# A graph network kernel: score factors stored once and doubled by the loads, and the projection stage in another order

## The chip, the cores and the metric

The kernel runs on one core of a Trainium2 chip. The metric is the device time of one execution in microseconds (us); before the change the median of three runs is 1293.65 us (1293.31 to 1293.77).

## The reference, cut to what matters

3125 nodes with 96 channels pass through four blocks, each added to its input. The change touches the first block, attention along the edges, and what feeds it. All four blocks start with the same layer norm and a ReLU:

```python
h = jnp.maximum(_layernorm(x, axis=-1), 0.0)
x = x + _L0_gnn_ref(h, qW, kW, vW, src, dst)
# _L0_gnn_ref: 4 heads of 24 channels, one row per edge
q = (embeds[rows] @ qW).reshape(e, HEADS, dh)
k = (embeds[cols] @ kW).reshape(e, HEADS, dh)
v = (embeds[cols] @ vW).reshape(e, HEADS, dh)
scores = jnp.clip(jnp.einsum('ehd,ehd->eh', q, k), -10.0, 10.0)
exp_s = jnp.exp(scores)
norms = jax.ops.segment_sum(exp_s, rows, num_segments=nvar)[rows]
w = exp_s / (norms + 1e-08)
res = jax.ops.segment_sum(w[:, :, None] * v, rows, num_segments=nvar).reshape(nvar, d)
return embeds + res
```

The kernel doesn't gather edges here. It has a matrix CT that counts the edges between each pair of nodes, forms the scores of all pairs, and weighs the exponentials with the counts. The column sums of CT (the degrees) are needed by later blocks and by the edge softmax.

## The kernel before, in words

Five engines run their own instruction streams, written out by hand; between stages all five meet (`meet`), so a stage ends for everybody when its last engine, or the last transfer that SyncE waits for, is done. The stages are: build (CT is made), projection, attention, propagation, last. Nothing in the streams is reordered by a planner: within an engine the order is that of the calls in `proj_tensor`, `proj_scalar`, `proj_vector` and `proj_sync`, and semaphores tie the engines together.

Projection works on 7 blocks of 512 nodes (the last has 64), of 4 tiles of 128 nodes each. Its pieces, with their lines in the kernel before:

- `dst_rows(b)` (L872): 25 matmuls sum CT's columns of block b into a PSUM bank; `rows(b)` on ScalarE (L811) copies it out; `dst_sums(b)` (L880) turns it to one column a tile in bank 6. After the seventh, `keep_degrees` (VectorE) copies the degrees, two matmuls (L916, L917) make running sums, and `last_edges` (L758 to L771, VectorE) makes an index of them.
- the layer norm on VectorE: `stats` (L704), `variances` (L709, L711) for all 25 tiles at once, the square root on ScalarE (L837, which needs a table load), the reciprocal (L788), and `norm(b)` (L717 and L720), which makes hb and adds ReLU(h) to X.
- `turn(b)` (L862) transposes hb to channels by nodes; `h_copy(b)` (L817, ScalarE) keeps it with the ReLU.
- `scales` (VectorE, L726 to L746) finds a power of two for the weights from `w_norm` (L903) and writes wqk.
- `products(b)`: Q and K of block b (L890), the values (L896).
- each Q or K block is split in a high fp16 part (`highs`, ScalarE, L825) and a low one, the rest (`low`, VectorE, L777). The score matmul contracts over 96 rows: 4 groups of 24, whose products are high·high, high·low, low·high and low·low. So DRAM holds four parts of each block, and `store` (L669, SyncE) writes each part twice: 4 transfers a block of 192 KB, Q ordered high, high, low, low, K ordered high, low, high, low. QH has two buffers: `highs(b)` waits until the stores of block b-2 have landed.
- X with ReLU(h) goes to DRAM (x1_d) in two stores (L682), after block 0 and after block 4.

Attention has 7 destination blocks by 25 source tiles, 175 steps. SyncE loads Q of a block (`q_load`, L1004) and K of each step (`k_load`, L1011) into a ring of three. One step is four score matmuls (L1064), ScalarE's exponentials (L1115 to L1119), floor and cap on GpSimd and VectorE (L982, L1144, L1150), and four value matmuls (L1074).

Of the kernel before, what the change touches and what calls it, by code (L numbers as in the profile page):

```python
# [4 lines left out]
F32 = mybir.dt.float32  # L5
# [645 lines left out]
def proj_sync(q, K):  # L651
# [13 lines left out]
    q.dma_start(K.wv4[:, :], K.vW).then_inc(S("wv4_in"), 16)  # L665
    def store(to, b, n, i):

        wb = width(b)
        q.dma_start(to.rearrange("r c h w -> (c h) r w")[:, :, 0:wb], bcast_out(K.QH[:, b % 2, n, i, 0:wb], 2, wb)  # L669
                    ).then_inc(S("q_out%d" % (b % 2)), 16)  # L670

    for b in range(7):
        q.wait_ge(S("q_low"), 2 * b + 1)
        for i in range(2):
            store(K.qd[b, 2 * i:2 * i + 2], b, 0, i)
        q.wait_ge(S("q_low"), 2 * b + 2)
        for i in range(2):
            store(K.kd[b, i:4:2], b, 1, i)
# [5 lines left out]
    q.wait_ge(S("q_out0"), 64 * 4)  # L684
    q.wait_ge(S("q_out1"), 64 * 3)


def proj_vector(v, K):
# [16 lines left out]

    def variances():
        v.wait_ge(step, own.n)
        for t in range(NT):
            v.bn_aggr(K.mv[:, t, :], K.bns[:, t, :]).then_inc(step, own.up())  # L709
        v.wait_ge(step, own.n)  # L710
        v.tensor_scalar(K.rs[:, 0, :], K.mv[:, :, 1], 1e-5, None, ALU.add).then_inc(S("ln0_var"), 1)  # L711

    def norm(b):

        sl = slice(4 * b, 4 * b + tiles(b))
        for t in range(4 * b, 4 * b + tiles(b)):
            c = v.tensor_scalar(K.hb[:, t, :], K.X[:, t, :], K.mv[:, t, 0:1], K.rs[:, 2, t:t + 1], ALU.subtract, ALU.mult)  # L717
        c.then_inc(S("h0"), 1)
        v.wait_ge(S("h0"), b + 1)
        v.scalar_tensor_tensor(out=K.X[:, sl, :], in0=K.hb[:, sl, :], scalar=0.0, in1=K.X[:, sl, :], op0=ALU.max, op1=ALU.add  # L720
                               ).then_inc(S("x1"), 1)

    def scales():

        v.wait_ge(S("w_norm"), 1)
        v.tensor_reduce(sc[:, 0, :], K.bank(3)[:, 0:192].rearrange("p (n c) -> p n c", n=2), AX.X, ALU.max  # L726
                        ).then_inc(step, own.up())
# [57 lines left out]
    variances()  # L785
    scales()
    v.wait_ge(S("ln0_std"), 1)
    v.reciprocal(K.rs[:, 2, :], K.rs[:, 1, :]).then_inc(step, own.up())  # L788
    v.wait_ge(step, own.n)
    norm(0)  # L790
    norm(1)
    norm(2)
# [11 lines left out]
def proj_scalar(a, K):  # L804
    S = K.S

    def rows(b):
        a.wait_ge(S("dst_rows"), b + 1)
        if b >= 2:
            a.wait_ge(S("dst_deg"), b - 1)  # L810
        a.activation(K.RD[:, b % 2, 0:width(b)], K.bank((7, 4)[b % 2])[:, 0:width(b)], ACT.Copy).then_inc(S("rows_kept"), 1)  # L811

    def h_copy(b):
        a.wait_ge(S("h_turned"), b + 1)
        if b >= 2:
# [20 lines left out]
    a.wait_ge(S("ln0_var"), 1)
    a.activation(K.rs[:, 1, :], K.rs[:, 0, :], ACT.Sqrt).then_inc(S("ln0_std"), 1)  # L837
    rows(3)
    rows(4)
    rows(5)  # L840
    h_copy(0)
    rows(6)
    h_copy(1)
    for b in range(7):
        highs(b)
        values(b)
        if b + 2 < 7:
            h_copy(b + 2)
    a.wait_ge(S("v_kept"), 7)


def proj_tensor(t, K):
    S, bank = K.S, K.bank

    def turn(b):
        t.wait_ge(S("h0"), b + 1)
        if b == 1:
            t.wait_ge(S("w_set"), 2)
        if b >= 2:
            t.wait_ge(S("hT"), b - 1)  # L860
        for i in range(tiles(b)):
            m = t.transpose(bank((0, 3)[b % 2])[0:96, 128 * i:128 * i + 128], K.hb[:, 4 * b + i, :], K.identf[:, :])  # L862
        m.then_inc(S("h_turned"), 1)

    def dst_rows(b):

        wb = width(b)
        if b >= 2:
            t.wait_ge(S("rows_kept"), b - 1)
        for a in range(NT):  # L870
            j = a % 4
            m = t.matmul(bank((7, 4)[b % 2])[32 * j:32 * j + 32, 0:wb], K.ones32[:, :], K.CT[:, a, 512 * b:512 * b + wb],  # L872
                         start=(a < 4), stop=(a >= NT - 4), tile_position=(0, 32 * j))
        m.then_inc(S("dst_rows"), 1)
# [9 lines left out]
    def products(b):  # L884
# [9 lines left out]
        for i in range(tiles(b)):  # L894
# [24 lines left out]
    turn(2)  # L919
    for b in range(1, 7):  # L920
        products(b)
        if b + 2 < 7:
            turn(b + 2)
    t.wait_ge(S("v_made"), 7)
# [118 lines left out]
def attn_tensor(p, K):  # L1043
# [966 lines left out]
```

## Time and profile before

| | us |
|---|---|
| median of the three runs | 1293.65 |
| profiled execution, device time | 1290.73 |
| span of its trace | 1288.6 |
| PE, DVE, ACT, POOL busy | 1040.7, 967.3, 692.3, 598.5 |
| projection stage | from 358.3 to 406.9 |
| attention stage | from 406.9 to 874.3 |

PE is the matmul engine (TensorE), PEld its weight loads, DVE VectorE, ACT ScalarE, POOL GpSimd, SP SyncE, which only issues transfers here. The profiled execution is 2.9 us shorter than the median of the runs. The projection is 3.8% of the span, so the shares of the page say little on it: it has to be read from windows of its own.

### The profile page before, as it was taken

How to read it: one execution, taken by the hardware profiler on the slowest of the kernel's cores; microseconds unless marked ns; L12 is line 12 of the kernel's file. 1: busy time of each engine (PE TensorE's matmuls, PEld its weight loads, DVE VectorE, ACT ScalarE, POOL GpSimd, SP SyncE). 2: the span in 40 equal slices, each digit the busy share in tenths (PEclk: the TensorE clock that was granted, in tenths of full speed). 3: DMA queues.
4: the chain of work that ended last, by engine and by line, in shares of the span. 5: the costliest groups of instructions: out<-in, count | busy, mean ns of one | idle time of the engine just before them, and what ended most of it. 6: DMA issues, size and time to landing. Idle time of an engine off the chain costs nothing.

```text
span 1288.6 us, 23338 instructions
## 1 busy us (share of the span) xinstructions
PE 1040.7 (81%) x8352; PEld 615.1 (48%) x8352; DVE 967.3 (75%) x1603; ACT 692.3 (54%) x903; POOL 598.5 (46%) x343
## 2 busy tenths in 40 slices
PE   3877777777795888888888888882799699999893
PEld 2545545544452222222222222221469699999783
DVE  8668888897764999999999999981865654542566
ACT  7555566556534997999989999980000000001221
POOL 8542453232001998999999899996000000000000
PEclk9988888999987998999999999996799899999996
DMA  0010000000027111121111222211000100010201
GB/s 10 28 39 5 5 9 5 6 7 16 1 63 213 35 36 46 44 54 41 42 47 45 51 54 50 53 41 46 1 1 32 37 29 21 2 33 8 71 25 38
DMA packets 98907, 44.80 MB, mean 35 GB/s; under 512 B 85196, under 2 KB 96716, under 8 KB 98672
## 3 DMA queue, kind: packets, MB, share of 16 engines
q1 hardware_dynamic: 97104, 41.58, 12.2%
q0 software_dynamic: 1696, 1.74, 0.5%
q8 instruction: 74, 1.21, 0.4%
q14 instruction: 33, 0.27, 0.1%
HBM read 30.73 MB, written 12.56 MB: 34 GB/s over the span
## 4 chain that ended last, share of the span: by engine, by line
PE 51%; DVE 25%; issue 11%; ACT 5%; POOL 5%; another core or an unknown queue 2%; DMA 2%; SPq 1%; DVEq 0%; ACTq 0%; POOLq 0%
PE PS L1325 16%; DVE Eb L1150 16%; PE PS L553 10%; PE PS L557 8%; POOL Eb L982 3%; PE PS L1765 3%; DVE Eb L1144 3%; PE PS L1333 2%; PE PS L1074 2%; ACT Eb L1115 2%; PE PS L1064 2%; PE PS L1316 1%; ACT Eb L1117 1%; PE PS L1772 1%
## 5 line engine op out<-in xcount | busy, mean ns | idle before, releaser
L982 POOL TENSOR_SCALAR Eb<-Eb 128x1024 f32<-128x1024 f32 (+4 forms) x175 | 431.2, 2486 | 77.1 <-ACT Eb L1119 75.8
L1150 DVE SCALAR_TENSOR_TENSOR Eb<-Eb,PS 128x1024 f32<-128x1024 f32 (+4 forms) x350 | 366.6, 1084 | 18.0 <-ACT Eb L1117 11.7
L1119 ACT ACTIVATE Eb<-PS,small 128x1024 f32<-128x1024 f32 (+2 forms) x263 | 251.7, 998 | 28.9 <-PE PS L1064 25.2
L593 ACT ACTIVATE CT<-PS 128x500 f32 x313 | 183.6, 587 | 141.2 <-PE PS L557 132.6
L553 PE MATMUL PS<-mov,oneS 128*128 128x100 f16 x1565 | 182.2, 226 | 79.6 <-issue 74.0
L553 PEld LDWEIGHTS PS<-mov,oneS 128*128 128x128 f16 x1565 | 144.7, 104 | 157.9 <-issue 111.5
L1325 PE MATMUL PS<-hs,CT 128*128 128x192 f16 (+1 forms) x2500 | 213.9, 247 | 3.5 <-DVE SG L1566 1.6
L1325 PEld LDWEIGHTS PS<-hs,CT 128*128 128x128 f16 (+1 forms) x2500 | 208.4, 99 | 7.4 <-DVE SG L1566 2.3
L1064 PE MATMUL PS<-Qb,Kb 96*128 96x512 f16 (+3 forms) x700 | 184.5, 367 | 10.4 <-ACT Eb L1119 6.7
L1074 PE MATMUL PS<-Eb,V 128*25 128x512 f32 (+3 forms) x1400 | 172.6, 566 | 3.4 <-DVE Eb L1150 1.8
L435 DVE TENSOR_TENSOR oneS<-iotaX,KL 128x2560 f16<-128x2560 int16 x80 | 120.8, 1510 | 68.7 <-PE PS L557 67.0
L1064 PEld LDWEIGHTS PS<-Qb,Kb 96*128 96x128 f16 (+1 forms) x700 | 45.3, 99 | 200.1 <-ACT Eb L1119 148.9
L557 PE MATMUL PS<-CT,identb 128*128 x313 | 137.7, 440 | 1.3 <-ACT CT L593 0.9
L1053 PE MATMUL PS<-identb,CT 128*128 128x128 f16 (+1 forms) x625 | 68.9, 225 | 59.7 <-DVE Eb L1150 51.4
L1053 PEld LDWEIGHTS PS<-identb,CT 128*128 128x128 f16 (+1 forms) x625 | 39.1, 100 | 129.1 <-DVE Eb L1150 114.3
L435 DVE TENSOR_TENSOR mov<-iotaM,KL 128x2000 f16<-128x2000 int16 x80 | 98.2, 1228 | 0.0
L1115 ACT ACTIVATE Eb<-PS,small 128x1024 f32<-128x1024 f32 (+4 forms) x87 | 95.1, 1093 | 0.0
L1117 ACT ACTIVATE Eb<-Eb,small 128x1024 f32<-128x1024 f32 (+4 forms) x87 | 90.7, 1043 | 2.8
L217 POOL TENSOR_SCALAR key<-hi 120x128 f32<-120x128 int32 x14 | 8.8, 630 | 173.8 <-DVE hi L444 173.7
L1446 ACT ACTIVATE hs<-PS 96x96 f32<-96x96 f32 x9 | 2.2, 248 | 138.8 <-PE PS L1357 138.8
L1566 DVE TENSOR_REDUCE SG<-PS 128x96 f32<-128x192 f32 (+1 forms) x75 | 24.8, 352 | 60.7 <-PE PS L1325 60.4
L1144 DVE TENSOR_SCALAR Eb<-Eb 128x1024 f32<-128x1024 f32 (+4 forms) x88 | 63.2, 718 | 7.4 <-ACT Eb L1119 7.4
(278 smaller groups left out, 1007.2 us busy)
## 6 DMA issues: line engine op xcount, KB each, us to landing
Kb<-kd SPq DMA_DIRECT2D x168, 96.0 KB, 2.3
qd<-QH SPq DMA_DIRECT2D x12, 192.0 KB, 2.9
kd<-QH SPq DMA_DIRECT2D x12, 192.0 KB, 3.2
hs<-t_d SPq DMA_DIRECT2D x12, 192.0 KB, 2.5
Qb<-qd SPq DMA_DIRECT2D x4, 384.0 KB, 3.9
CT<-x_d SPq DMA_DIRECT2D x1, 1200.0 KB, 9.1
x_d<-B SPq DMA_DIRECT2D x6, 192.0 KB, 1.9
t_d<-A SPq DMA_DIRECT2D x6, 192.0 KB, 1.9
```

Source lines behind the costliest of these rows:

```text
L435: return v.tensor_tensor(out.rearrange("p e (c two) -> p e c two", two=2), v_in, k_in, ALU.is_equal)
L553: t.matmul(to, K.oneS[:, s % DEEP, o + k, :], K.mov[:, s % DEEP, o + k, :].rearrange("p (a w) -> p a w", a=25), start=(k == 0), stop=False ...
L557: t.matmul(ps, K.identb[:, :], K.CT[:, :, bass.ds(vals[0], GI * W)], start=False, stop=True, skip_group_check=True).then_inc(S("counted"), 1)
L593: a.activation(K.CT[:, :, bass.ds(words[g % 4][0], GI * W)], K.bank(g % 4)[:, 0:25 * GI * W].rearrange("p (a c) -> p a c", a=25), ACT.Copy ...
L982: g.tensor_scalar(e, e, ELO, None, ALU.max).then_inc(S("floored"), 1)
L1053: m = p.transpose(K.cntv[it % 2][0:r, 128 * i:128 * i + w], K.CT[0:w, B0[b] + i, 128 * t:128 * t + r], K.identb[0:w, 0:w])
L1064: m = p.matmul(bank(h)[0:r, 0:wb], K.Kb[:, it % NK, h, 0:r], K.Qb[:, b % 2, h, 0:wb], start=True, stop=True)
L1074: m = p.matmul(bank(4)[32 * h:32 * h + 25, 0:wb], K.V[0:r, t, h, :], K.Eb[0:r, (2 * it + h // 2) % NE_, h % 2, 0:wb], start=(t == 0), stop ...
L1115: a.activation(e, ps, ACT.Relu, bias=K.ten[0:r, 0:1], scale=K.unsc[0:r, :]).then_inc(S("score_read"), 1)
L1119: a.activation(e, ps, ACT.Exp, scale=K.unsc[0:r, :]).then_inc(S("score_read"), 1)
L1150: v.scalar_tensor_tensor(out=e, in0=e, scalar=EHI, in1=cn, op0=ALU.min, op1=ALU.mult).then_inc(S("weighed"), 1)
L1325: m = p.matmul(bank(t % FIRST)[0:r, 0:w], K.CT[:, a, 128 * t:128 * t + r], hs[:, a, :, :].rearrange("p k d -> p (k d)"), start=(a == 0), s ...
```

## The change

1. DRAM holds two parts of each Q or K block instead of four: the high once and the low once (`qd`, `kd` of 7 x 2 x 24 x 4 x 512). A block is stored in 2 transfers of 192 KB, not 4.
2. The loads make the doubling: Q in four transfers of 24 partitions a piece, not one of 96, K in two of 48 partitions a step, not one of 96. A wait for K is for 32 and not 16.
3. QH has three buffers.
4. The layer norm goes in three portions (tiles 0 to 3, 4 to 11, 12 to 24), each with its own variances, square root and reciprocal. hb is a ring of 16 tiles.
5. The column sums are placed between the blocks' products on TensorE, with one PSUM bank (3), not two; the transposes have bank 0 alone.
6. `scales` comes after `norm(0)`; `keep_degrees` and `last_edges` come behind `low(4)`; the two x1 stores come after blocks 3 and 6.

The core of the diff:

```diff
-    K.hb = sb(st, "hb", [128, NT, D], F32)
+    K.hb = sb(st, "hb", [128, 16, D], F32)
-    K.QH = sb(st, "QH", [96, 2, 2, 2, 512], F16)
+    K.QH = sb(st, "QH", [96, QH_DEEP, 2, 2, 512], F16)
...
+QH_DEEP = 3
-    def store(to, b, n, i):
+    def store(to, b, n):
-        q.dma_start(to.rearrange("r c h w -> (c h) r w")[:, :, 0:wb], bcast_out(K.QH[:, b % 2, n, i, 0:wb], 2, wb)
-                    ).then_inc(S("q_out%d" % (b % 2)), 16)
+        q.dma_start(to.rearrange("i c h w -> (c h) i w")[:, :, 0:wb], K.QH[:, b % QH_DEEP, n, :, 0:wb]
+                    ).then_inc(S("q_out%d" % (b % QH_DEEP)), 16)
-        if b in (0, 4):
-            lo, hi = (0, 12) if b == 0 else (12, NT)
-            q.wait_ge(S("x1"), 3 if b == 0 else 7)
+        if b in (3, 6):
+            lo, hi = (0, 12) if b == 3 else (12, NT)
+            q.wait_ge(S("x1"), 3 if b == 3 else 7)
...
     stats(0)
+    variances(0)
     v.wait_ge(S("w_in"), 32)
     v.tensor_tensor(K.wsq[:, :, :], wr, wr, ALU.mult).then_inc(S("w_sq"), 1)
+    deviations(0)
+    norm(0)
+    scales()
     stats(1)
+    variances(1)
+    deviations(1)
+    norm(1)
+    low(0)
+    norm(2)
     stats(2)
...
+    low(4)
     keep_degrees()
+    norm(6)
     last_edges()
-    for b in range(7):
-        low(b)
-        if b + 3 < 7:
-            norm(b + 3)
+    low(5)
+    low(6)
...
+    deviation(0)
     rows(0)
+    h_copy(0)
+    deviation(1)
+    highs(0)
     rows(1)
+    values(0)
+    h_copy(1)
+    deviation(2)
+    highs(1)
...
+    for b in (1, 2):
+        dst_rows(b)
+        turn(b)
+        dst_sums(b)
+        products(b)
+    for b in (3, 4):
+        dst_rows(2 * b - 3)
+        turn(b)
+        dst_sums(2 * b - 3)
+        dst_rows(2 * b - 2)
+        products(b)
+        dst_sums(2 * b - 2)
...
-            q.dma_start(K.Qb[:, b % 2, :, o:o + w], K.qd[c // 512].rearrange("r c h w -> (r c) h w")[:, :, c % 512:c % 512 + w]
-                        ).then_inc(S("q_in%d" % (b % 2)), 16)
+            for r in range(4):
+                q.dma_start(K.Qb[24 * r:24 * r + 24, b % 2, :, o:o + w], K.qd[c // 512, r // 2, :, :, c % 512:c % 512 + w]
+                            ).then_inc(S("q_in%d" % (b % 2)), 16)
...
-        q.dma_start(K.Kb[:, it % NK, :, 0:r], K.kd[t // 4].rearrange("r c h w -> (r c) h w")[:, :, 128 * (t % 4):128 * (t % 4) + r]
-                    ).then_inc(S("k_in%d" % (it % NK)), 16)
+        kt = K.kd[t // 4].rearrange("i c h w -> (i c) h w")[:, :, 128 * (t % 4):128 * (t % 4) + r]
+        for i in range(2):
+            q.dma_start(K.Kb[48 * i:48 * i + 48, it % NK, :, 0:r], kt).then_inc(S("k_in%d" % (it % NK)), 16)
```

ScalarE at the start of the projection, kernel before: RD is the copied column sums, rs the square root's tile, hTb the turned block, and the brackets name the semaphores waited for.

```order
L811 ACTIVATE RD<-PS 128x512 [waits placed,dst_rows,meet]
L811 ACTIVATE RD<-PS 128x512 [waits dst_rows]
L811 ACTIVATE RD<-PS 128x512 [waits dst_deg,dst_rows]
L837 ACT_TABLE_LOAD
L837 ACTIVATE rs<-rs 128x25 [waits ln0_var]
```

The same place now (L859 is the square root, L834 the copy of the sums, L840 `h_copy`, L848 `highs`):

```order
L859 ACT_TABLE_LOAD [waits placed,ln0_var]
L859 ACTIVATE rs<-rs 128x4 [waits meet]
L834 ACTIVATE RD<-PS 128x512 [waits dst_rows]
L840 ACTIVATE hTb<-PS 96x512 [waits h_turned]
L859 ACTIVATE rs<-rs 128x8 [waits ln0_var]
L848 ACTIVATE QH<-PS 96x512 [waits q_made] x2
```

The table load stood by itself and waited for nothing; now it is the first instruction of the stage and carries the wait for the first variances. Each later square root stands ahead of a `highs`.

VectorE at the stage's end, now (L764 and L766 are `keep_degrees`, L731 and L734 `norm(6)`, L772 to L785 `last_edges`, L791 `low`):

```order
L764 COPY small<-PS 128x24 [waits dst_deg]
L766 COPY small<-PS 64x1 [waits step_v]
L731 TENSOR_SCALAR hb<-X,mv,rs 128x96 [waits h_turned]
L734 SCALAR_TENSOR_TENSOR X<-hb,X 128x96 [waits h0]
L772 COPY bns<-PS 128x25 [waits deg_sum]
L773 COPY bns<-PS 128x25
L785 TENSOR_SCALAR msk<-small 128x25
L791 TENSOR_TENSOR QH<-PS,QH 96x512 [waits q_high] x2
L791 TENSOR_TENSOR QH<-PS,QH 96x64 [waits q_high] x2
```

Before, the degrees and the index were done ahead of the first `low`; now they stand ahead of the last two, behind a wait for TensorE.

SyncE around the meeting, now (L675 is `store`, L686 the x1 store, L1046 `q_load`, L1055 `k_load`):

```order
L675 DMA qd<-QH 96x2x64 [waits q_low]
L675 DMA kd<-QH 96x2x64 [waits q_low]
L686 DMA x_d<-X 128x1248 [waits x1]
L1046 DMA Qb<-qd 24x2048 [waits q_out2,q_out1,x1_out,q_out0,meet]
L1046 DMA Qb<-qd 24x2048 x3
L1055 DMA Kb<-kd 48x4x128 x6
```

The larger x1 store has become the stage's last transfer, and the first K load now has four Q issues ahead of it instead of one.

## Rows read from the trace of the kernel before

**Rows 1.** Windows of the projection: PE, PEld, DVE, ACT, POOL busy, clock, DMA, GB/s.

```profile
358.00:364.00 6.00, 5.21 (x51) 2.23 (x51) 2.43 (x18) 0.84 (x2) 0.50 (x2) 0.59 0.74 189
364.00:384.00 20.00, 20.00 (x217) 13.72 (x217) 14.37 (x84) 9.13 (x16) 0.00 (x0) 1.00 0.04 11
384.00:397.00 13.00, 11.58 (x57) 6.90 (x57) 9.98 (x25) 6.54 (x14) 0.00 (x0) 1.00 0.90 277
397.00:407.00 10.00, 1.75 (x14) 1.32 (x13) 1.71 (x7) 1.92 (x6) 0.00 (x0) 0.67 0.81 247
```

**Rows 2.** Waits in the projection: us in total, times, longest.

```profile
ACT QH L825 <- DMA kd<-QH: 6.0, 4, 2.5
```

**Rows 3.** Transfers issued in the projection: count, KB each, us to landing.

```profile
qd<-QH SPq DMA_DIRECT2D x12, 192.0 KB, 2.9
x_d<-X SPq DMA_DIRECT2D x1, 624.0 KB, 5.0
wv<-in_L_gnn_vW SPq DMA_DIRECT2D x1, 36.0 KB, 4.3
```

**Rows 4.** Timeline of TensorE in the projection: start, us, engine, line.

```profile
358.79 5.18 PE L872 MATMUL PS<-CT,ones 128*32 128x512 f16 x50 [1.25 <-DVE sel L695]
...
365.21 1.69 PE L872 MATMUL PS<-CT,ones 128*32 128x512 f16 x25
366.82 1.05 PE L880 MATMUL PS<-sel,RD 128*128 128x1 f32 x8
...
381.00 0.62 PE L862 MATMUL PS<-identf,hb 128*96 128x128 f32 x4
381.46 1.88 PE L890 MATMUL PS<-hTb,wqk 96*96 96x512 f32 x4
383.18 1.03 PE L896 MATMUL PS<-wv,hTb 96*128 96x96 f32 x8
```

**Rows 5.** Timeline of ScalarE: the table loads and what follows one.

```profile
367.55 1.28 ACT L837 ACT_TABLE_LOAD   x1
...
411.88 1.28 ACT L1119 ACT_TABLE_LOAD   x1 [9.60 <-PE PS L1064]
413.18 1.11 ACT L1119 ACTIVATE Eb<-PS,small 128x1024 f32<-128x1024 f32 x1
```

**Rows 6.** Timeline of VectorE in the projection.

```profile
360.74 0.74 DVE L704 BATCH_NORM_STATS2 bns<-X 128x6 f32<-128x96 f32 x4 [1.76 <-DMA X<-in_x]
...
370.47 0.35 DVE L726 TENSOR_REDUCE sc<-PS 128x2 f32<-128x192 f32 x1
...
372.07 0.51 DVE L742 TENSOR_SCALAR wqk<-wr,sc 96x96 f32<-96x96 f32 x2
...
373.09 1.05 DVE L717 TENSOR_SCALAR hb<-X,mv,rs 128x96 f32<-128x96 f32 x4
...
381.20 0.18 DVE L758 COPY bns<-PS 128x25 f32<-128x25 f32 x1 [2.90 <-PE PS L917]
...
382.61 1.28 DVE L777 TENSOR_TENSOR QH<-PS,QH 96x512 f16<-96x512 f32 x2
```

**Rows 7.** Timeline of SyncE after the meeting.

```profile
406.87 0.32 SPq L1004 DMA_DIRECT2D Qb<-qd  x1
407.23 1.97 SPq L1011 DMA_DIRECT2D Kb<-kd  x3
```

**Rows 8.** Timeline of TensorE: the first scores.

```profile
410.75 1.89 PE L1064 MATMUL PS<-Qb,Kb 96*128 96x512 f16 x4 [1.80 <-DMA Kb<-kd]
```

**Rows 9.** Transfers of the whole run: count, KB each, us to landing.

```profile
Kb<-kd SPq DMA_DIRECT2D x168, 96.0 KB, 2.3
x_d<-B SPq DMA_DIRECT2D x6, 192.0 KB, 1.9
```

**Rows 10.** Waits of SyncE in attention: us in total, times, longest.

```profile
SPq L1011 <- PE PS L1064: 323.9, 165, 6.6
```

**Rows 11.** Score matmuls: count, ns min/median/max, first and last start.

```profile
L1064 PE MATMUL PS<-Qb,Kb x700: 298/379/634, 410.8 to 864.0; 96*128 96x512 f16 x96, 96*128 96x384 f16 x48, 96*128 96x320 f16 x24, 96*64 96x512 f16 x4
```

More of the change, by code:

```diff
@@ L704, in stats, with variances, deviations @@
             v.bn_stats(K.bns[:, t, :], K.X[:, t, :]).then_inc(step, own.up())
-    def variances():
+    def variances(i):
+        lo, hi = X_IN[i]
         v.wait_ge(step, own.n)
-        for t in range(NT):
+        for t in range(lo, hi):
             v.bn_aggr(K.mv[:, t, :], K.bns[:, t, :]).then_inc(step, own.up())
         v.wait_ge(step, own.n)
-        v.tensor_scalar(K.rs[:, 0, :], K.mv[:, :, 1], 1e-5, None, ALU.add).then_inc(S("ln0_var"), 1)
+        v.tensor_scalar(K.rs[:, 0, lo:hi], K.mv[:, lo:hi, 1], 1e-5, None, ALU.add).then_inc(S("ln0_var"), 1)
+    def deviations(i):
+        lo, hi = X_IN[i]
+        v.wait_ge(S("ln0_std"), i + 1)
+        v.reciprocal(K.rs[:, 2, lo:hi], K.rs[:, 1, lo:hi]).then_inc(step, own.up())
+        v.wait_ge(step, own.n)
     def norm(b):
         sl = slice(4 * b, 4 * b + tiles(b))
+        ring = slice(4 * (b % 4), 4 * (b % 4) + tiles(b))
+        if b >= 4:
+            v.wait_ge(S("h_turned"), b - 3)
         for t in range(4 * b, 4 * b + tiles(b)):
-            c = v.tensor_scalar(K.hb[:, t, :], K.X[:, t, :], K.mv[:, t, 0:1], K.rs[:, 2, t:t + 1], ALU.subtract, ALU.mult)
+            c = v.tensor_scalar(K.hb[:, t % 16, :], K.X[:, t, :], K.mv[:, t, 0:1], K.rs[:, 2, t:t + 1], ALU.subtract, ALU.mult)
         c.then_inc(S("h0"), 1)
         v.wait_ge(S("h0"), b + 1)
-        v.scalar_tensor_tensor(out=K.X[:, sl, :], in0=K.hb[:, sl, :], scalar=0.0, in1=K.X[:, sl, :], op0=ALU.max, op1=ALU.add
+        v.scalar_tensor_tensor(out=K.X[:, sl, :], in0=K.hb[:, ring, :], scalar=0.0, in1=K.X[:, sl, :], op0=ALU.max, op1=ALU.add
                                ).then_inc(S("x1"), 1)
@@ L776, in low @@
             v.wait_ge(S("q_high"), 2 * b + n + 1)
-            v.tensor_tensor(K.QH[:, b % 2, n, 1, 0:wb], K.bank(qk_bank(b, n))[0:96, 0:wb], K.QH[:, b % 2, n, 0, 0:wb],
+            v.tensor_tensor(K.QH[:, b % QH_DEEP, n, 1, 0:wb], K.bank(qk_bank(b, n))[0:96, 0:wb], K.QH[:, b % QH_DEEP, n, 0, 0:wb],
                             ALU.subtract).then_inc(S("q_low"), 1)
     stats(0)
+    variances(0)
     v.wait_ge(S("w_in"), 32)
     v.tensor_tensor(K.wsq[:, :, :], wr, wr, ALU.mult).then_inc(S("w_sq"), 1)
+    deviations(0)
+    norm(0)
+    scales()
     stats(1)
-    stats(2)
[L785 to L792, printed above, removed]
+    variances(1)
[3 more added lines that the diff above has]
+    norm(2)
+    stats(2)
+    variances(2)
+    low(1)
+    deviations(2)
+    norm(3)
+    low(2)
+    norm(4)
+    low(3)
+    norm(5)
+    low(4)
     keep_degrees()
+    norm(6)
     last_edges()
-    for b in range(7):
-        low(b)
-        if b + 3 < 7:
-            norm(b + 3)
+    low(5)
+    low(6)
     v.wait_ge(S("q_low"), 14)
@@ L816, in h_copy @@
             a.wait_ge(S("v_made"), b - 1)
-        a.activation(K.hTb[:, b % 2, 0:width(b)], K.bank((0, 3)[b % 2])[0:96, 0:width(b)], ACT.Relu).then_inc(S("hT"), 1)
+        a.activation(K.hTb[:, b % 2, 0:width(b)], K.bank(0)[0:96, 0:width(b)], ACT.Relu).then_inc(S("hT"), 1)
     def highs(b):
@@ L831, in values, with deviation @@
                      K.bank(5)[0:r, 0:96 * n].rearrange("p (k c) -> p k c", c=24), ACT.Copy).then_inc(S("v_kept"), 1)
+    def deviation(i):
+        lo, hi = X_IN[i]
+        a.wait_ge(S("ln0_var"), i + 1)
+        a.activation(K.rs[:, 1, lo:hi], K.rs[:, 0, lo:hi], ACT.Sqrt).then_inc(S("ln0_std"), 1)
+    deviation(0)
     rows(0)
+    h_copy(0)
+    deviation(1)
+    highs(0)
     rows(1)
+    values(0)
+    h_copy(1)
+    deviation(2)
+    highs(1)
     rows(2)
[L836 to L844, printed above, removed]
-        highs(b)
-        values(b)
-        if b + 2 < 7:
-            h_copy(b + 2)
+    values(1)
+    h_copy(2)
+    highs(2)
+    for b in (3, 4):
+        rows(2 * b - 3)
+        values(b - 1)
+        h_copy(b)
+        rows(2 * b - 2)
+        highs(b)
+    for b in (5, 6):
+        values(b - 1)
+        h_copy(b)
+        highs(b)
+    values(6)
     a.wait_ge(S("v_kept"), 7)
@@ L856, in turn @@
         t.wait_ge(S("h0"), b + 1)
[L857 to L860, printed above, removed]
+        if b:
+            t.wait_ge(S("hT"), b)
         for i in range(tiles(b)):
-            m = t.transpose(bank((0, 3)[b % 2])[0:96, 128 * i:128 * i + 128], K.hb[:, 4 * b + i, :], K.identf[:, :])
+            m = t.transpose(bank(0)[0:96, 128 * i:128 * i + 128], K.hb[:, 4 * (b % 4) + i, :], K.identf[:, :])
         m.then_inc(S("h_turned"), 1)
@@ L900, in proj_tensor @@
     dst_rows(0)
-    dst_rows(1)
     t.wait_ge(S("w_sq"), 1)
-    t.matmul(bank(3)[:, 0:192], K.ones96[:, :], K.wsq[:, :, :].rearrange("p n c -> p (n c)"), start=True, stop=True
+    t.matmul(bank(7)[:, 0:192], K.ones96[:, :], K.wsq[:, :, :].rearrange("p n c -> p (n c)"), start=True, stop=True
              ).then_inc(S("w_norm"), 1)
-    for b in range(2, 7):
-        dst_sums(b - 2)
-        dst_rows(b)
     turn(0)
-    dst_sums(5)
-    turn(1)
-    dst_sums(6)
+    dst_sums(0)
+    t.wait_ge(S("w_set"), 2)
     t.wait_ge(S("wv4_in"), 16)
     products(0)
+    for b in (1, 2):
[3 more added lines that the diff above has]
+        products(b)
+    for b in (3, 4):
+        dst_rows(2 * b - 3)
[4 more added lines that the diff above has]
+        dst_sums(2 * b - 2)
+    turn(5)
+    products(5)
+    turn(6)
     t.wait_ge(S("tri"), 1)
@@ L918, in proj_tensor @@
              ).then_inc(S("deg_sum"), 1)
[L919 to L923, printed above, removed]
+    products(6)
     t.wait_ge(S("v_made"), 7)
@@ L970, in q_loaded @@
 def q_loaded(b):
-    return 16 * sum(len(list(q_pieces(i))) for i in range(b % 2, b + 1, 2))
+    return 64 * sum(len(list(q_pieces(i))) for i in range(b % 2, b + 1, 2))
 def attn_gpsimd(g, K):
```

30 lines of the change are left out of this document (14 added, 16 removed).

## The prediction

> **What bounds the kernel now.** The change lies in one stage and its seam to the next, so I read windows first. From 364 to 384 TensorE is busy 20.00 of 20 us while DMA moves 11 GB/s; from 384 on DMA is busy 90% at 277 GB/s, and in the last ten microseconds TensorE works 1.75 [rows 1]. The projection thus has two halves with different limits: first TensorE (column sums), then the stores of the score factors. The waits name the second: ScalarE's `highs` stand 6.0 us, in four waits, for stores of two blocks earlier to land [rows 2]. Six full blocks bring 24 stores of 192 KB, of which the Q half is one row [rows 3]. The stage ends at 406.87, when SyncE issues the first load [rows 7], and the first score starts at 410.75, having waited for K [rows 8].
>
> **The stores: what they can give.** Half of them go: 12 of 192 KB for the six full blocks, 2.3 MB, 8.3 us at 277 GB/s [rows 1]. But the gain ends where another engine ends. TensorE's work in the stage is 5.21 + 20.00 + 11.58 + 1.75 = 38.5 us [rows 1], from 358.8 on [rows 4], so 397.3 without a gap. So a gain of some 5 us after a tail of 4 us is what a dense TensorE would allow, and the question is whether the new order keeps it dense. It doesn't at its start, as the following shows.
>
> **The start.** Before, `products(0)` stood behind all column sums, so VectorE's norm and weight scaling had 19 us. Now they stand before it. The first statistics end at 361.48 [rows 6]; four aggregations and the addition of the 1e-5 take about 0.5, so 362.0. There ScalarE's table load begins, because it now carries the wait for the variances; it takes 1.28 and was hidden before [rows 5]. Square root about 0.2, reciprocal 0.2: `norm(0)` starts at 363.8. It takes 1.05 for the tiles and 0.56 for X. Then `scales`: from its first reduction at 370.47 to the start of wqk at 372.07 are 1.6, and two scalings 0.4 [rows 6]. The weights are set at 367.4. Vw is not later: issued near 362.3, it takes 4.3 [rows 3]. TensorE meanwhile has the first sums of columns (until 361.4: 25 of the 50 matmuls that take 5.18), the weight norm, one transposition and one `dst_sums`, at the low clock some 2.8 us of the 6.0 between 361.4 and 367.4. It idles over 3 us, where it idled nowhere before.
>
> **The rest of TensorE's chain.** Durations by start to start, at the high clock: `dst_rows` 1.61, `dst_sums` 0.98 (its row shows 1.05 with the end overlapped), a turn 0.46, Q and K 1.72 [rows 4]; values 0.87 (the row's 1.03 less the 0.16 by which the 1.88 of Q and K runs over too). Left after 367.4: six full products 15.5 and the small one 0.6; five and a bit `dst_rows` 8.4; sums 5.2; turns 2.5; the degree products 0.4 (half a `dst_sums`). Sum 32.6. To that come waits for ScalarE: with one bank for the turn and one for the sums, `dst_sums` follows its rows' copy (0.6) with only a turn to cover it, 0.3 in each of four blocks, and `products(5)` waits 0.8 for its own `h_copy`, the last 0.2. Sum 2.1. The clock: in the window 358 to 364 it is 0.59 (mostly 1.2 GHz), and 1.00 (2.4 GHz) after it; 50 matmuls at the low level took 5.18 where 25 at the high took 1.61 [rows 1, 4]. It was low while those first 50 ran, 358.8 to 364.0. I take a low stretch as long again once work is dense, 367.4 to near 372: half of it, 2.3, is lost. TensorE ends at 367.4 + 32.6 + 2.1 + 2.3 = 404.4. The blocks' stores are far from that: two of 192 KB in 6 to 8 us.
>
> **The tail.** `last_edges` waits for the degree products, which stand just before the last products, so they end at 403.6. It takes 1.41 (381.20 to 382.61), and behind it on VectorE wait `low(5)` and `low(6)`, 1.28 and 0.3 [rows 6]: 406.6. Behind these on SyncE are the last three stores, each about 0.45 to issue, and then the x1 store of 624 KB, issued at 407.7. It took 5.0 to land before, in a full queue [rows 3]; 192 KB in an empty one takes 1.9 [rows 9], and 432 KB more at 277 GB/s 1.6: 3.5, between 3.0 and 5.0. The stage would end at 411.2. The same layout by hand for the old order puts `products(0)` 0.4 later than the trace has it; I take that off: 410.8, against 406.87: **+3.9** (+1 to +8).
>
> **The start of attention.** Before, the Q load (0.32) and K loads of 0.66 each preceded a first score 3.88 after the first issue [rows 7, 8]. Now K's two halves stand behind four Q issues: 0.32 and three of 0.43 to 0.6, then 0.6 twice. The last one needed is issued 1.3 to 2.2 later than before; four transfers also deliver sooner in part. I take **+1.5** (+0.7 to +2.5), near the low end, since empty queues show 0.32.
> The Trainium skill, "DMA: Bandwidth & Descriptors", section "Why a DMA increments its semaphore by 16 and not by 1", says that a transfer uses the largest number of engines up to 16 that divides its slowest dimension: 12 for 24 partitions, where 96 had 16. No row here shows one of 24; by it the Q loads would last a third longer, at most 0.5 more, inside the range given.
>
> **Attention itself.** A step lasts (864.0 - 410.8) / 174 = 2.60 us [rows 11]. SyncE waits 323.9 us in 165 of its K issues, 1.96 each [rows 10]. The second K issue (0.6) fits. A load goes out three steps before its use, 7.8, and needs 1.2 to issue and 2.3 to land [rows 9], so 3 us are to spare even when a Q load of four or eight issues (2 to 4 us) comes between; with eight, in the narrow blocks, about one may show. I take 0, up to +3.
>
> **Other edits at nothing.** Three QH buffers: the two-block distance is now over 12 us against a landing of 3, the third buffer is never needed. The smaller hb ring waits for turns four blocks old. The first x1 store lies beside products.
>
> **A rule that speaks against this working.** A table load in the trace takes 1.28 and the exponential starts 0.02 after its end [rows 5]. The Trainium skill, "ScalarE: Activation LUTs", section "What ACT_TABLE_LOAD costs", adds a drain of 1.38. By it `products(0)` and the sum would move by another 1.4; the trace doesn't show a drain here, so I leave it out.
>
> **Sum.** 3.9 + 1.5 = 5.4. On the profiled execution, 1290.73, that is 1296.1; the runs' median is 2.9 above it, and 1293.65 + 5.4 = **1299.1**.
>
> **Rivals.**
> *A, faster: TensorE stays dense.* If norm, weights and copies came as TensorE needed them, it would end at 397.3, the tail (two stores, x1) at 401.7, and with +1.5 at the seam the kernel would gain 3.7: 1290.0. For it: the halved stores free 8 us that the waits prove. Against: the weights at 367.4 rest on five rows. It decides when idle at the start falls below about 1 us and `last_edges` ends before `highs(5)`. 0.07.
> *B, no change that can be measured.* The order costs as laid out, but clock and tail each come out at their kind ends (no cold products 2.3, the x1 store in 3.0, seam 0.7): 5.4 - 2.3 - 0.5 - 0.8 = 1.8, 1295.5. 0.14.
> *C, slower by more: the low clock holds.* The stage's new order leaves short pauses in each block. If the clock rises only near 380, another 4 us: 1303. For it: the low clock at this same place before, and 0.67 where work is thin [rows 1]. Against: after 367.4 hardly a pause is over 0.3. 0.11.
> *D, K loads late in attention.* If the doubled issues and the Q bursts use up the 3 us, each of six block changes shows 0.5 to 1: 1303 too. Against: the 1.96 of slack in each step. 0.06.
> *Forecast* 0.62, own range 1297 to 1301.5.
>
> The measurement of this kernel can tell about 0.2%, 2.6 us, from no change. Faster is A: 0.07; the same is B: 0.14; slower is the forecast with C and D: 0.79. The range for 8 in 10 reaches from 1295 (into B) to 1303.5.
>
> **What would show it.** In the new trace: the table load starting near 362 behind the variances; `products(0)` starting near 367.4 with TensorE idle some 3 us before it; a clock below 1 until about 372; TensorE ending near 404, two `low` blocks behind `last_edges`, an x1 store as the last transfer; `highs` no longer waiting for any store; the first attention issue near 410.8 and the first score 5.4 after it. A first issue at or before 406.9 would refute the stage's part, a score less than 4 after the first issue the seam's.

## The result, and the profile after

The changed kernel takes 1298.82 us in the median of six runs, against 1293.48 for the kernel before on the same chip: a ratio of 1.0049 (95% interval 1.0036 to 1.0061), 5.3 us slower. The prediction was 1299.1. All ratios here are of fast runs; this leaves out one run of the experiment "changed, filled", which took 4942 us.

The profiled execution took 1297.89 (span 1296.0). One cut of the trace into stages runs through all that follows: the projection from its first load of X to the first load of Q, the seam from there to the first score, attention from there to the next stage's first load.

| us | before | after | |
|---|---|---|---|
| build, up to the first load of X | 358.32 | 357.44 | -0.88 |
| projection | 48.55 | 55.31 | +6.76 |
| seam | 3.88 | 4.52 | +0.64 |
| attention | 463.59 | 464.42 | +0.83 |
| the rest | 414.26 | 414.31 | +0.05 |

The windows of the projection answer to [rows 1], with the same columns:

```profile
358.00:364.00 6.00, 4.06 (x27) 1.43 (x26) 2.64 (x16) 1.97 (x3) 0.04 (x1) 0.50 0.81 216
364.00:384.00 20.00, 19.58 (x113) 11.88 (x114) 15.77 (x78) 6.23 (x13) 0.00 (x0) 0.70 0.15 41
384.00:397.00 13.00, 12.77 (x126) 7.69 (x124) 5.78 (x14) 5.44 (x11) 0.00 (x0) 1.00 0.33 105
397.00:407.00 10.00, 8.68 (x73) 5.82 (x72) 3.31 (x16) 5.36 (x13) 0.00 (x0) 1.00 0.16 44
```

DMA, busy 90% from 384 to 397 before, is at 33%, and TensorE is at work to the end, where it had 1.75 of ten microseconds. TensorE's sum of busy time in these windows grew from 38.5 to 45.1 for the same work, mainly since it ran longer at the low clock. The timeline of TensorE shows where (to be read beside [rows 4]):

```profile
357.91 3.15 PE L907 MATMUL PS<-CT,ones 128*32 128x512 f16 x25 [1.25 <-DVE sel L699]
361.65 1.01 PE L937 MATMUL PS<-wsq,ones 96*128 96x192 f32 x2 [0.60 <-DVE wsq L797]
364.27 1.09 PE L897 MATMUL PS<-identf,hb 128*96 128x128 f32 x4 [1.61 <-DVE hb L731]
365.15 1.71 PE L915 MATMUL PS<-sel,RD 128*128 128x1 f32 x8
366.90 3.73 PE L925 MATMUL PS<-hTb,wqk 96*96 96x512 f32 x4
370.42 1.86 PE L931 MATMUL PS<-wv,hTb 96*128 96x96 f32 x8
372.21 3.17 PE L907 MATMUL PS<-CT,ones 128*32 128x512 f16 x25
375.31 0.97 PE L897 MATMUL PS<-identf,hb 128*96 128x128 f32 x4
376.11 1.00 PE L915 MATMUL PS<-sel,RD 128*128 128x1 f32 x8
376.98 1.94 PE L925 MATMUL PS<-hTb,wqk 96*96 96x512 f32 x4
...
402.21 1.96 PE L925 MATMUL PS<-hTb,wqk 96*96 96x512 f32 x4 [0.68 <-ACT hTb L840]
...
405.71 0.55 PE L925 MATMUL PS<-hTb,wqk 96*96 96x64 f32 x4 [0.22 <-ACT hTb L840]
```

The same Q and K products take 3.73 at 366.90 and 1.94 at 376.98; the column sums of block 1 (372.21) take 3.17, where 25 such matmuls took 1.69 at the high clock before. Windows date the rise of the clock (columns as above, the granted clock third from the end):

```profile
368.00:372.00 4.00, 4.00 (x12) 2.34 (x10) 3.58 (x20) 1.28 (x3) 0.00 (x0) 0.50 0.02 6
372.00:376.00 4.00, 4.00 (x31) 1.60 (x30) 3.97 (x19) 0.58 (x2) 0.00 (x0) 0.50 0.35 98
376.00:380.00 4.00, 4.00 (x30) 2.70 (x32) 2.51 (x18) 2.31 (x6) 0.00 (x0) 1.00 0.00 0
```

So TensorE stood at 1.2 GHz (0.50) up to 376, 18.6 us into the stage. Before, it left that level 4.5 us into it, near 362.9: the 0.59 of the window from 358 to 364 [rows 1] is 4.9 us at 0.50 and 1.1 at 1.00. ScalarE's start shows the table load behind the wait for the variances (compare [rows 5]):

```profile
361.42 1.28 ACT L859 ACT_TABLE_LOAD   x1 [4.06 <-DVE rs L716]
362.72 0.21 ACT L859 ACTIVATE rs<-rs 128x4 f32<-128x4 f32 x1
```

And the stage's end, VectorE and then SyncE (compare [rows 6, 7]):

```profile
405.54 0.18 DVE L772 COPY bns<-PS 128x25 f32<-128x25 f32 x1 [3.62 <-PE PS L962]
...
406.95 1.54 DVE L791 TENSOR_TENSOR QH<-PS,QH 96x512 f16<-96x512 f32 x4
```

```profile
407.65 0.30 SPq L675 DMA_DIRECT2D qd<-QH  x1
408.25 0.30 SPq L675 DMA_DIRECT2D kd<-QH  x1
408.60 0.48 SPq L675 DMA_DIRECT2D qd<-QH  x1
409.12 0.48 SPq L675 DMA_DIRECT2D kd<-QH  x1
409.65 0.45 SPq L686 DMA_DIRECT2D x_d<-X  x1
412.75 1.52 SPq L1046 DMA_DIRECT2D Qb<-qd  x4
414.31 3.88 SPq L1055 DMA_DIRECT2D Kb<-kd  x6
```

`last_edges` starts when the degree products are done (405.54), the last two blocks' `low` come behind it, and the x1 store closes the stage; all engines wait for it. Among the waits of the stage none is left of `highs` for a store. The largest of TensorE's waits are the ones in brackets above.

### The profile page after: what moved, and what is told of

Read it like the earlier page. It is cut to its first block, busy times and chain, and to the rows that moved or that the text cites. A ratio compares the mean times of both kernels' runs of the same rounds, so it can differ in the third digit from the quotient of the medians.

```text
span 1296.0 us, 23530 instructions
## 1 busy us (share of the span) xinstructions
PE 1047.7 (81%) x8352; PEld 617.8 (48%) x8352; DVE 967.1 (75%) x1607; ACT 693.3 (54%) x905; POOL 598.0 (46%) x343
## 4 chain that ended last, share of the span: by engine, by line
PE 50%; DVE 26%; issue 11%; ACT 5%; POOL 5%; another core or an unknown queue 2%; DMA 1%; SPq 0%; DVEq 0%; ACTq 0%; POOLq 0%
DVE Eb L1193 16%; PE PS L1368 16%; PE PS L553 10%; PE PS L557 7%; POOL Eb L1023 3%; DVE Eb L1187 3%; PE PS L1808 3%; PE PS L1376 2%; PE PS L1117 2%; ACT Eb L1158 2%; PE PS L1107 2%; PE PS L1359 1%; ACT Eb L1160 1%; PE PS L925 1%
```

## The experiments

Each kernel is compared with the kernel before on the same chip. The stage lengths come from one profile each. The build stage, the same in all of these, lasted from 357.4 to 362.9 in thirteen profiles, so whole times differ by microseconds that have nothing to do with the change; the projection of the changed kernel was 55.31 and 55.77 in two profiles. What varies in it is the moment at which the clock rises: 16.6 to 19.5 us into the stage in the five profiles that share the changed kernel's start. Half of that span, about 1.5 us, is an estimate of how far such a stage can move by itself.

| | ratio to before (95%) | projection | seam | attention |
|---|---|---|---|---|
| before | | 48.55 | 3.88 | 463.6 |
| changed | 1.0049 (1.0036 to 1.0061) | 55.31 | 4.52 | 464.4 |
| old order, parts once | 0.9978 (0.9962 to 0.9994) | 42.35 | 4.54 | 462.8 |
| changed, filled | 1.0056 (1.0034 to 1.0078) | 52.36 | 4.64 | 462.3 |
| changed, table first | 1.0051 (1.0034 to 1.0068) | 53.50 | 4.55 | 462.5 |
| changed, tail | 1.0034 (1.0013 to 1.0056) | 51.39 | 4.56 | 464.8 |
| changed, old storage | 1.0058 (1.0040 to 1.0077) | 57.30 | 3.91 | 460.7 |
| changed, two buffers | one run | 54.73 | 4.60 | 462.4 |
| changed, all three mended | 1.0021 (1.0003 to 1.0039) | 50.18 | 4.55 | 462.1 |
| the same, and unlocked | 0.9988 (0.9967 to 1.0010) | 45.83 | 4.46 | 462.6 |
| changed, again | one run | 55.77 | 4.49 | 464.2 |
| old order and three edits | 0.9970 (0.9953 to 0.9988) | 41.36 | 5.08 | 466.4 |
| old order, exponential first | 0.9939 (0.9916 to 0.9963) | 41.69 | 4.57 | 461.2 |

### One part alone: the storage in the old order

This is the kernel before with the halves stored once; the same is done for kd, and `q_load` and `k_load` are those of the change.

```diff
-        for i in range(2):
-            store(K.qd[b, 2 * i:2 * i + 2], b, 0, i)
+        store(K.qd[b], b, 0)
```

> The kernel before in its own order, with only the storage changed: each part stored once (2 stores of 192 KB a block), doubled by the loads (four for Q, two for K); two QH buffers, x1 stores after blocks 0 and 4 as before. Theory (the storage gains, the new order loses more): no highs waits for a store, TensorE ends the projection near 399.5, the last low near 401, the stage ends near 403.5 instead of 406.9, so 3.4 less; the seam costs 0.6 and attention 0.8 more, as measured after the change; together 2.0 less than before: ratio to before about 0.9985. Rival (the doubled loads cost what the stores give, the order is not to blame): ratio 1.002 or more, with the stage ending near 406 or attention longer by several us.

The stage fell by 6.2 us where 3.4 were expected, and the time by 0.2%, where 0.15% was expected. The first theory holds and the rival falls: the storage alone makes the kernel a little faster. The waits of its projection say what became of [rows 2]:

```profile
ACT QH L823 <- DMA kd<-QH: 0.6, 1, 0.6
```

### The clock: extra matmuls in TensorE's first pauses

```diff
+    def fill(n):
+        for a in range(n):
+            t.matmul(bank(4)[0:32, :], K.ones32[:, :], K.CT[:, a, 0:512], start=True, stop=True)
     dst_rows(0)
+    fill(6)
     t.wait_ge(S("w_sq"), 1)
...
+    fill(14)
     turn(0)
```

> The changed kernel with 20 extra matmuls on TensorE whose result nobody reads (six before the weight norm, fourteen after it), in the pauses at the start of the projection. Theory (low clock after a broken start): the granted clock reaches 1.00 some 7 to 10 us sooner, before 370 instead of 376; products(0) and the next column sums take 2.6 and 1.6 instead of 5.3 and 3.1; the stage is 3 to 4.5 us shorter, ratio to the changed kernel near 0.997. Rival (the stage is set by VectorE's chain and the waits, not by the clock): the clock rises but the stage stays within 1 us. Second rival: these fillers do not raise the clock and put products(0) later by up to 1 us.

The stage is 2.95 shorter, at the low end of what was expected, although the twenty matmuls, over 5 us long, put `products(0)` 1.1 later. Windows of its stage, which starts at 360.46:

```profile
363.00:365.00 2.00, 2.00 (x12) 0.73 (x5) 1.47 (x10) 0.64 (x1) 0.00 (x0) 0.50 0.94 227
365.00:367.00 2.00, 2.00 (x9) 0.83 (x8) 1.07 (x5) 1.33 (x3) 0.00 (x0) 0.93 1.06 295
367.00:369.00 2.00, 2.00 (x11) 0.89 (x10) 1.79 (x8) 0.00 (x0) 0.00 (x0) 1.00 0.04 9
```

The clock is up 4.8 us into the stage (0.93 is 0.3 us at 0.50), about as in the kernel before, and near 14 sooner than in the changed one. From the start of `products(0)` to that of the last values TensorE takes 35.2 (10.6 to 45.8 of the stage) and not 39.3 (9.5 to 48.8): the low clock cost the changed kernel 4.0 us. In the time of the whole nothing shows (1.0056 beside 1.0049): 3 us are below what these runs resolve, so this verdict rests on the trace.

### The table load ahead of the wait

```diff
+    a.activation(K.rs[:, 1, NT - 1:NT], K.identf[:, 0:1], ACT.Sqrt)
     deviation(0)
```

> The changed kernel with one more square root of one column ahead of the first wait for the variances, whose result is overwritten later, so that the table load doesn't wait for them. Theory: the load runs near 357.5 beside other work, the first square root and with it norm(0), the weights and products(0) come 1.3 us sooner, and the stage ends 1 to 1.5 us sooner (up to 2 if the clock also rises sooner): about 0.999 of the changed kernel. Rival: products(0) waits for something else (the load of Vw, 365.0), and nothing is gained.

```profile
366.61 3.73 PE L926 MATMUL PS<-hTb,wqk 96*96 96x512 f32 x4
```

The stage starts at 358.41, so `products(0)` came at 8.20 of it and not 9.46: 1.26 sooner, which is the load. The wait for Vw, the rival, didn't bind. The stage lost 1.8; the half microsecond beyond 1.26 is no more than the clock's rise moves between profiles. Again the whole time doesn't resolve it.

### The tail

```diff
-    last_edges()
     low(5)
     low(6)
+    last_edges()
...
     for b in range(7):
+        if b == 5:
+            x1_store(b)
```

> The changed kernel with last_edges behind low(6) and the second x1 store ahead of the stores of block 5. Theory (the tail is serial: last_edges 1.4, three store issues, an x1 store of 3.0): low(5) no longer waits for the degree products, the last transfer is a store of 24 KB that lands in 2.0; TensorE's end stays at 406.6, the last low comes 1.4 sooner at about 407.1, the stage ends 2.5 to 3 us sooner: about 0.998 of the changed kernel. Rival (the stores of blocks 5 and 6 now queue behind the x1 store of 624 KB): less than 1 us.

3.9 shorter, where 2.5 to 3 were expected. Counted from the stage's start, the last small store is issued 2.0 sooner, and what closes the stage is now a store of 24 KB:

```profile
407.46 0.30 SPq L675 DMA_DIRECT2D qd<-QH  x1
...
407.81 0.45 SPq L675 DMA_DIRECT2D kd<-QH  x1
...
409.50 1.52 SPq L1051 DMA_DIRECT2D Qb<-qd  x4
```

It lands 1.6 after its issue, the x1 store 3.0 after its own. The time points the same way, 1.0034 beside 1.0049, but these intervals overlap: this verdict rests on the trace too.

### The storage undone in the new order

```diff
-        store(K.qd[b], b, 0)
+        for i in range(2):
+            store(K.qd[b, 2 * i:2 * i + 2], b, 0, i)
...
-        K.qd, K.kd = dram("qd", 7, 2, 24, 4, 512, dt=F16), dram("kd", 7, 2, 24, 4, 512, dt=F16)
+        K.qd, K.kd = dram("qd", 7, 4, 24, 4, 512, dt=F16), dram("kd", 7, 4, 24, 4, 512, dt=F16)
```

> The changed kernel with only the storage put back: four stores of 192 KB a block and one load for Q, one for K, the rest (three buffers, norm in portions, column sums between the blocks) as changed. Theory (in the new order the stores have 6 to 8 us a block and bind nothing): the projection stage stays within 1 us of the changed kernel's 55.3, perhaps 0.5 to 1.5 longer at its end where two blocks' stores and the x1 store meet; the seam is 3.9 instead of 4.5; the time equals the changed kernel's within 1.5 us. Rival (halving the stores is worth its 6 us in any order): the stage is 58 us or longer.

The edit puts `store`, `q_load`, `k_load` and the sizes of qd and kd back and leaves the rest. The stage is 2.0 longer, the seam 0.6 shorter, the time the same. The rival, that the storage is worth its 6 us in any order, is wrong: in this order it is worth 2.0. TensorE's last values end 49.1 us into the stage in both, so all of it lies at the end, where the stores of the last two blocks and x1 queue up. The seam's 3.91 beside 4.5 in ten other profiles prices the doubled first loads at 0.6.

### Two buffers

```diff
-QH_DEEP = 3
+QH_DEEP = 2
```

> The changed kernel with two QH buffers instead of three. Theory: block b's highs come over 12 us after those of b-2 and the stores land in 2.2, so nothing waits; the stage stays at 55.3 within 0.5 (the last small block may wait 0.3). Rival: highs wait for stores and the stage grows by over 1 us.

54.73, no longer than with three, and in its trace no `highs` waits for a store: the third buffer does nothing here. The 0.6 by which the stage is shorter goes with the clock, which rose 16.6 us into it and not 18.6. The time, 1298.98, is one run.

### All three mendings

The changed kernel with the table load ahead, the tail, and six of the extra matmuls in three places:

```diff
+    a.activation(K.rs[:, 1, NT - 1:NT], K.identf[:, 0:1], ACT.Sqrt)
...
+    fill(1)
     t.wait_ge(S("w_sq"), 1)
...
+    fill(3)
...
+    fill(2)
```

> The changed kernel with all three mendings at once: the table load ahead of the wait, six extra matmuls in TensorE's first pauses (one, three and two), last_edges behind low(6) and the second x1 store ahead of block 5's stores. Theory (the causes add up, table and clock in part the same): stage 55.3 - 3.9 (tail) - 1.8 (table) - 2.5 (clock) = 47.1, near the 48.55 of the kernel before, the time within 2 us of before. It stays about 5 us longer than the old order with the parts stored once (42.35), because of TensorE's pauses at the start and its waits for ScalarE's copies. Rival (they overlap almost wholly): 51 us.

50.18: neither theory. First TensorE with its pause, then ScalarE, then windows of the same kernel:

```profile
379.53 1.68 PE L913 MATMUL PS<-CT,ones 128*32 128x512 f16 x25
381.14 0.64 PE L903 MATMUL PS<-identf,hb 128*96 128x128 f32 x4
383.08 1.05 PE L921 MATMUL PS<-sel,RD 128*128 128x1 f32 x8 [1.30 <-ACT RD L839]
384.00 2.85 PE L931 MATMUL PS<-hTb,wqk 96*96 96x512 f32 x4
386.64 1.86 PE L937 MATMUL PS<-wv,hTb 96*128 96x96 f32 x8
388.44 3.17 PE L913 MATMUL PS<-CT,ones 128*32 128x512 f16 x25
```

```profile
381.37 0.21 ACT L864 ACTIVATE rs<-rs 128x13 f32<-128x13 f32 x1 [4.68 <-DVE rs L721]
```

```profile
383.00:385.00 2.00, 1.92 (x11) 1.36 (x12) 1.93 (x7) 0.89 (x3) 0.00 (x0) 0.97 0.62 176
385.00:387.00 2.00, 2.00 (x5) 0.91 (x4) 0.89 (x2) 0.70 (x2) 0.00 (x0) 0.50 0.06 21
...
391.00:393.00 2.00, 1.94 (x16) 1.16 (x11) 0.00 (x0) 1.36 (x3) 0.00 (x0) 0.82 0.00 0
```

Being faster at the start, TensorE reached `dst_sums(2)` before ScalarE had copied the sums: ScalarE waited 4.68 for the third variances, ahead of `highs(1)` and that copy. This is the lock that the next experiment takes out. 1.8 us after the end of the pause of 1.30 the clock fell, and it stayed down for 6.8 us (384.9 to 391.7, by the 0.97 and the 0.82), so part of what the first mendings had won was given back.

### And unlocked

```diff
     h_copy(1)
-    deviation(2)
     highs(1)
     rows(2)
     values(1)
+    deviation(2)
     h_copy(2)
```

> The changed kernel with the three mendings of before (table load, extra matmuls, tail) and one more: on ScalarE the third square root stands behind highs(1), the copy of the third column sums and the values, and no longer ahead of them. In the kernel without this, TensorE paused 1.3 us before dst_sums(2) for that copy and its clock then went from 1.00 to 0.50 for 5.7 us. Theory: without the pause the clock doesn't fall; the stage goes from 50.2 to about 46.5 (1.3 of pause and 2.8 of the low clock less), the time 3.5 us less, about the time before. Rival: the pause was not what brought the clock down: then only 1 us is won and the low stretch stays somewhere in the stage.

```profile
375.00:380.00 5.00, 4.89 (x43) 2.76 (x42) 4.74 (x27) 2.03 (x5) 0.00 (x0) 1.00 0.27 78
380.00:385.00 5.00, 4.89 (x58) 3.15 (x60) 2.89 (x7) 2.17 (x5) 0.00 (x0) 1.00 0.30 82
385.00:400.00 15.00, 14.20 (x131) 8.68 (x124) 5.53 (x14) 6.71 (x13) 0.00 (x0) 1.00 0.39 135
```

45.83: 4.35 less, where 3.7 were expected, with the clock at 1.00 from 365 to 400, the windows shown and those before them. The pause and the second fall of the clock went together, and the rival, that 1 us is won and the low stretch stays, falls. It is one profile each, on two chips. So the changed order, mended in four places, is 2.7 shorter than the stage before, and its time equals before's within the interval.

### The changed kernel again

> The changed kernel once more, to see how far one profile repeats: stage within 0.5 us of 55.3 if the clock's behaviour repeats, seam 4.5, attention within 2 us of 464.4, and the build stage, which differs by 3 us between profiles of kernels that share it, anywhere from 357 to 361.

55.77 and 55.31: the long low clock repeats, on another chip too (up to 19.5 us into the stage). The time is one run, 1286.72, against a median of 1278.0 for the kernel before on that chip.

### A better kernel than both

It is the old order with the parts once, and three edits: three buffers for the halves (hb becomes a ring of 16 tiles, so that they fit), the layer norm of block 3 ahead of the degrees, and the first Q load issued from ScalarE's queue and not from SyncE's.

```diff
-    K.QH = sb(st, "QH", [96, 2, 2, 2, 512], F16)
+    K.QH = sb(st, "QH", [96, 3, 2, 2, 512], F16)
-    K.hb = sb(st, "hb", [128, NT, D], F32)
+    K.hb = sb(st, "hb", [128, 16, D], F32)
     keep_degrees()
+    norm(3)
     last_edges()
...
 def attn_scalar(a, K):
+    q_load(a, K, 0)
```

> The kernel before in its own order with each part stored once and doubled by the loads, and three more edits: three QH buffers with hb as a ring of 16 tiles, norm(3) ahead of last_edges, and the first Q load issued by ScalarE beside SyncE's first K loads. Theory: against the same order without these three, the stage loses the wait of turn(3) (0.7) and of block 5's highs (0.6), so 41.3 instead of 42.35; the seam goes from 4.5 to about 3.8, since K's first two issues no longer stand behind four Q issues; together 1.7 less, about 1287.3 or 0.9965 of before. Rival: TensorE's own work sets the stage and the transfers' landing the seam: within 0.5 of the kernel without the three edits.

The stage came out as expected (41.36), the seam didn't: 5.08, where 3.8 was expected. The first score now waited for Q:

```profile
404.25 2.03 ACTq L1005 DMA_DIRECT2D Qb<-qd  x4
...
409.33 1.86 PE L1068 MATMUL PS<-Qb,Kb 96*128 96x512 f16 x4 [2.97 <-DMA Qb<-qd]
```

Issued from a second queue beside K's loads, four Q issues took 2.03 instead of 1.52, and the first score came 3.0 after the last of them. That edit is a loss and was taken back; in its place came what the table load of the projection taught:

```diff
 def attn_scalar(a, K):
+    a.activation(K.small[:, 150:151], K.identf[:, 0:1], ACT.Exp)
```

> The kernel before in its own order with each part stored once, three QH buffers, hb as a ring and norm(3) ahead of last_edges, the first Q load issued by SyncE again, and one exponential of one element ahead of the first wait for scores, so that its table load of 1.28 us doesn't stand between the first scores and the first exponential. Theory: stage 41.4, seam 4.5, and from the first score to the end of attention 1.2 us less than the 462.3 to 464.8 of the others; time about 1.7 us below the same order without these edits, ratio to before about 0.9955. Rival: attention is bound by VectorE and GpSimd alone, which don't get their first work sooner in a way that lasts: nothing.

```profile
402.18 1.28 ACT L1110 ACT_TABLE_LOAD   x1
404.48 0.20 ACT L1110 ACTIVATE small<-identf 128x1 f32<-128x1 f32 x1 [1.02 <-SPq L71]
```

The load lies in the wait for the last stores, and attention lasted 461.2, the shortest of all with doubled loads. The first exponential starts 1.13 after the first score (410.22, 409.09); before, 2.43 lay between them (413.18, 410.75) [rows 5, 8]. So the load is off that path. Ratio 0.9939 (0.9916 to 0.9963), the lowest of the study. How much of the step from 0.9970 is the exponential's can't be read from it: the two intervals touch, the seam's edit was taken back in the same step, and attention differs by over 2 us between kernels whose attention has the same instructions.

## Why the prediction was right

**What bound the kernel** (two halves, stores in the second): shown by the old order with the parts once, which is 6.2 shorter, close to the 5 that were said to be free. TensorE's last values end at 39.5 of that stage, as a dense TensorE was said to (397.3 less 358.3 is 39.0); what follows took 2.8 and not the 4 us that were allowed.

**The start.** Said: load at 3.7 of the stage, `products(0)` at 9.1. Measured 3.98 and 9.46. The price of the moved table load was shown by taking it away: 1.26. TensorE idled 2.2 in its pauses there (0.60 and 1.61) and not over 3, since its work in between took longer at the low clock than was laid out.

**The table load's drain.** The Trainium skill's "ScalarE: Activation LUTs", section "What ACT_TABLE_LOAD costs", adds 1.38 for a drain. Here the square root starts 0.02 after the load's end (361.42 + 1.28, 362.72): leaving it out was right for this case.

**The clock** was mis-sized. Said: low from 367.4 until near 372, 2.3 lost. Measured: low until 376; half of that dense stretch is 4.6, and the run with filled pauses puts the loss at 4.0. The step that failed is "a low stretch as long again". It was already misread: the first 50 matmuls did not all run at the low level. Before, the clock rose near 362.9, 4.1 us after TensorE's first matmul of the stage at 358.79, in the middle of them. And it did not repeat: in the changed kernel TensorE was busy 4.00 of 4 from 368 to 372 and again to 376 at 0.50, some 9 us of dense work from 366.90 on. That filling the first pauses brings the rise back to 4.8 us of the stage is shown; why the clock stayed low for so long under dense work is not, and stays open. The rise at 376 lies midway between the forecast's 372 and the 380 of rival C.

**TensorE's dense work** was mis-sized by about as much: 32.6 said. With the pauses filled and the clock up, `products(0)` to the end of the last values took 35.6, of which 1.4 are waits: 34.2. The high-clock rows used for the sum were those of the old order; in the new one a block's products take 2.73 from start to start and not 2.59, and a turn 0.64 and not 0.46.

**TensorE's waits for ScalarE**: 2.1 said, 1.2 measured: 0.68 before `products(5)`, 0.22 before the last, and gaps of 0.1 ahead of three `dst_sums`. Not seen in the prediction: that the third square root can hold up the copy for `dst_sums(2)`, which the low clock hid, and which appeared when the clock was mended.

**The tail** (last_edges, `low(5)`, `low(6)`, x1 store): said 6.8 from TensorE's end to the stage's (404.4 to 411.2), before 0.4 was taken off; measured 6.2 (406.6 to 412.75). The x1 store took 3.0, the low end of its bounds. Taking 0.4 off for the hand layout made the error of the stage larger.

**The seam**: +1.5 said, +0.6 measured. The second half of the first K load is issued 1.9 later than the first K load before, within the 1.3 to 2.2 that were said. What was missed is its landing: 2.2 after its issue, where the whole load took 3.5 before. The first score waited for K; the trace has no landing times for the Q loads of 24 partitions, so whether these are slower is not shown. **Attention**: 0 said, +0.8 in this pair; no K load after the first was waited for. With doubled loads it lasted 461.2 to 466.4, with single ones 460.7 and 463.6: whether they cost anything there stays open.

That 5.3 was measured where 5.4 was said is partly luck. The stage was foreseen 2.9 too short, the seam 0.9 too long, attention 0.8 too short: in the profiles the parts that the change touches add up to 8.2 us, and the profiled pair as a whole, whose build stage was 0.9 shorter by chance, to 7.2. The direction and the path are borne out: the late start of the products, the pauses, the low clock behind them, the tail closed by the x1 store. The exact size isn't.

**Where the expected gain went.** From the old order with the parts once (42.35) to the changed kernel (55.3) are 13.0 us. The tail is 3.9 of it, the other mendings and the moved square root together 5.6 (51.4 to 45.8), and 3.5 remain. TensorE's last values end 4.2 later there than in the old order (43.7 and 39.5 of the stage), while what follows them is 0.7 shorter. How the 4.2 divide among pauses, extra matmuls and waits for copies was not tested.

## What to carry to other kernels

Halving a transfer is worth what the next limit leaves: here 6.2 us in one order and 2.0 in another. When work is moved ahead of a long dense stretch of TensorE, count the pause twice, once as time and once as the slower clock behind it (here 2.2 us of pauses and 4.0 of clock). Look where the table load stands: where it stands behind the wait of its activation, as both do here, an activation of one element ahead of the wait hides it. Judge a change of a few microseconds in one stage by that stage's length in the trace and not by the whole.

## What was not expected of the hardware

- A pause of 1.30 us on a TensorE that had run at 1.00 for 14 us was followed, 1.8 us after its end, by 6.8 us at 0.50; without that pause the clock stayed at 1.00 until TensorE's work of the stage was done. A pause of 0.68 later in the same stage had no such effect.
- In the changed kernel the clock stayed at 0.50 through 9 us of dense work, where before it rose 4.1 us after TensorE's first column sums began.
- On one chip the part after attention lasted 400.3 to 400.7 in all three profiles, in the ten profiles from the other chips 414.3 to 415.2, with the same instructions. Ratios here are within a chip.
- Four Q loads took 2.03 us to issue from ScalarE's queue while SyncE issued K, and 1.52 from SyncE alone.
